# 32x32 turns on VectorE, and the residual added on GpSimd, in the second layer of a two-layer sequence kernel

## The reference, cut to what matters

```python
def _L1_cond_ref(x, c, weight, c_weight, bias):        # x (32,128,2048); 9 taps, 4 groups
    out = lax.conv_general_dilated(x, weight, (1,), [(4, 4)], ..., feature_group_count=4)
    return out + einsum('nd,od->no', c, c_weight)[:, :, None] + bias[None, :, None]
def _L1_ffn_ref(x, up, down, perm):                    # 16 heads of 128 positions, 512 wide inside
    t = x.reshape(b * l, Dm)[:, perm].reshape(b * l, 16, 128)
    t = gelu(einsum('bhd,hdm->bhm', t, up), approximate=False)
    t = einsum('bhm,hmd->bhd', t, down).reshape(b * l, 2048)
    return t[:, unperm]
x = x + _L0_ffn_ref(_L0_cond_ref(x, ...), ...)         # first layer: leaves x1
x = x + _L1_ffn_ref(_L1_cond_ref(x, ...), up, down, perm)
```

## Time and profile before

| | |
|---|---|
| median of 3 runs | 2582.73 us (2581.07 to 2588.96) |
| the profiled execution's own time | 2583.87 us |
| its span, first to last instruction | 2582.0 us |
| TensorE busy | 2528.0 us, 98% of the span |
| VectorE, ScalarE, GpSimd busy | 71%, 39%, 37% |
| second layer, convolution ahead of the heads | about 1470 to 1514 us |
| heads without a last addition | 16 steps, to about 1650 us |
| heads with convolution and last addition | 92 steps, to about 2426 us |
| heads without convolution (`late`) | to about 2548 us |
| last block's sum | to 2582 us |

### The profile page before, as it was taken

The page is one execution under the profiler, slowest core; times in us unless marked ns, Lnnn a source line. Parts: engine busy times, 40 slices in busy tenths (PEclk is TensorE's granted clock), DMA queues, the critical chain, the costliest instruction groups (busy, mean ns, idle before and its releaser), DMA issues.

```text
span 2582.0 us, 39106 instructions
## 1 busy us (share of the span) xinstructions
PE 2528.0 (98%) x12090; PEld 2099.3 (81%) x12090; DVE 1822.8 (71%) x2667; ACT 1001.8 (39%) x1632; POOL 950.8 (37%) x826
## 2 busy tenths in 40 slices
PE   8899999999999999999999999999999999999997
PEld 6788888888888888888888778888888888888775
DVE  6665555965556755576445768888888888888876
ACT  3221212321122322232222555555555555555573
POOL 2366645466654455233223212222222222222231
PEclk9999999999999999999999999999999999999998
DMA  9965644665545777576555754577767676777786
GB/s 318 322 196 199 201 168 155 238 210 197 196 163 185 228 229 228 161 250 210 160 165 186 223 153 131 170 219 219 221 214 226 205 223 205 225 226 223 212 281 240
DMA packets 417281, 541.02 MB, mean 210 GB/s; under 512 B 36248, under 2 KB 270064, under 8 KB 417072
## 3 DMA queue, kind: packets, MB, share of 16 engines
q1 hardware_dynamic: 314816, 307.40, 39.6%
q10 hardware_dynamic: 78144, 154.27, 15.9%
q0 software_dynamic: 24112, 76.80, 9.4%
HBM read 309.72 MB, written 228.61 MB: 208 GB/s over the span
## 4 chain that ended last, share of the span: by engine, by line
PE 91%; DVE 4%; DMA 2%; issue 2%; ACT 1%; ACTq 0%; SPq 0%; POOL 0%; DVEq 0%; POOLq 0%
PE ps_c L461 44%; PE ps_up L1398 13%; PE ps_y L1408 13%; PE ps_c L1423 9%; PE ps_v L439 4%; PE ps_c L427 2%; PE ps_zt L1436 2%; PE ps_f L1444 2%; DVE w_lo L1004 1%; PE ps_up L1423 1%; DVE ring_lo L951 0%; DVE r_early L1000 0%; DMA a_s<-in_lora_a 0%; DMA x_n<-in_up 0%; DMA aggw_d<-agg 0%
## 5 line engine op out<-in xcount | busy, mean ns | idle before, releaser
L461 PE MATMUL ps_c<-w_hi,ring_hi 128*128 128x512 f32 x1792 | 703.8, 393 | 3.8 <-DVE r_early L1000 3.2
L461 PE MATMUL ps_c<-w_hi,ring_lo 128*128 128x512 f32 x1792 | 698.0, 390 | 0.0
L461 PE MATMUL ps_c<-w_lo,ring_hi 128*128 128x512 f32 x1792 | 697.8, 389 | 0.0
L611 ACT ACTIVATE ring_hi<-raw_n 128x512 fp32r<-128x512 f32 x382 | 239.4, 631 | 848.7 <-DVE raw_n L942 235.1
L1380 POOL DMA_INDIRECT y_d<-y_s,idx x128 | 145.7, 1139 | 723.1 <-ACT y_s L1548 689.6
L1505 ACT ACTIVATE kern<-ps_up 128x512 f32<-128x512 f32 x512 | 306.6, 599 | 257.5 <-PE ps_up L1398 245.4
L461 PEld LDWEIGHTS ps_c<-w_hi,ring_hi 128*128 128x128 f32 x1792 | 336.7, 188 | 74.5 <-issue 4.0
L461 PEld LDWEIGHTS ps_c<-w_hi,ring_lo 128*128 128x128 f32 x1792 | 336.4, 188 | 70.2
L461 PEld LDWEIGHTS ps_c<-w_lo,ring_hi 128*128 128x128 f32 x1792 | 336.7, 188 | 67.3
L1622 DVE TENSOR_TENSOR g_lo<-kern,g_hi 128x512 fp32r<-128x512 f32 x512 | 354.5, 692 | 38.2 <-ACT g_hi L1509 21.8
L1000 DVE TENSOR_TENSOR r_early<-ps_c,r_early 128x512 f32<-128x512 f32 x256 | 176.6, 690 | 276.2 <-PE ps_c L461 276.2
(11 more groups left out here) (211 smaller groups left out, 3832.9 us busy)
## 6 DMA issues: line engine op xcount, KB each, us to landing
u_d<-raw_n ACTq DMA_DIRECT2D x64, 512.0 KB, 3.2
x_d<-r_early ACTq DMA_DIRECT2D x128, 256.0 KB, 3.6
raw_n<-u_d SPq DMA_DIRECT2D x64, 512.0 KB, 3.6
x_d<-x_s ACTq DMA_DIRECT2D x126, 256.0 KB, 2.7
u_s<-x_d SPq DMA_DIRECT2D x496, 64.0 KB, 2.2
z_d<-x_s SPq DMA_DIRECT2D x120, 256.0 KB
rear<-y_d SPq DMA_DIRECT2D x112, 256.0 KB
rear<-x_d SPq DMA_DIRECT2D x112, 256.0 KB, 4.0
```

The costliest lines, as they stand in the source:

```text
L461: mm = nc.tensor.matmul(bank, a[:, dc, :], w[k][:, dc, :], start=(first and dc == 0 and n == 0), stop=(dc == 3 and n == 2), skip_group_che ...
L611: nc.scalar.activation(ring_hi[g % RING][:].rearrange("p a n -> p (a n)"), factor(q, k, p), ACT.Copy).then_inc(hi_ready, 1)
```

## The change

TensorE's transposes in the loops of the second layer are taken out. VectorE transposes 32x32 squares in SBUF instead, straight from `z_s` into the tile (`turn_z`) and from the loaded y rows into `results` (`turn_y`). Since such a turn moves nothing between quadrants of partitions, three layouts change with it: the four units of a tile are now the four batches of one group, z and y rows are moved by four transfers of 32 partitions, and the output is written by phase in rows of 512 bytes and brought into order on the host. The addition of x1 becomes a GpSimd instruction, `add_x1`, between the gather and the scatter. For mc = 0 and 2 g_hi is now made by ScalarE in every step, for mc = 1 and 3 by VectorE. ScalarE's write of `z_s` now waits for `zt_ready`, VectorE's turn. VectorE takes `turn_y` before `turn_z`. The last block keeps TensorE's transposes; its 16 results leave in four stores each, two on SyncE and two on ScalarE. Cut to its core:

```diff
-        def by_scalar(k, h, mc):
-            return late(k, h) and mc % 2 == 1
+        def by_scalar(mc):
+            return mc % 2 == 0
@@ conv_unit, final_unit
-            return H * k + h + LEAD, h % 2, SB * k + (h + LEAD) // G, h % G
+            group, batch = divmod((h + LEAD) % H, SB)
+            return H * k + h + LEAD, h % 2, SB * k + SB * ((h + LEAD) // H) + batch, group
-            return H * (k - 1) + h, h % 2, SB * (k - 1) + h // 4, h % 4
+            return H * (k - 1) + h, h % 2, h // 4, h % 4
+        def final_part(dram, k, phase, q):
+            first = SB * (k - 1)
+            return dram[bass.ds(first, SB), :, phase, q * P:(q + 1) * P].rearrange("b c q -> c b q")
+        def z_rows(dram, r, part):
+            return dram.rearrange("(w i r) n -> r i w n", w=WIDE, r=S)[r, :, :, part * C:(part + 1) * C]
@@ load_final (SyncE)
-                sp.dma_start(yt_s[j], y_d[1 - parity][c * 512:(c + 1) * 512, h // 4 * C:(h // 4 + 1) * C]
-                             .rearrange("(l p) r -> p l r", p=P)).then_inc(yt_in[j], 16)
+                rows = y_d[1 - parity].rearrange("(q w i s) n -> q s i w n", q=4, w=4, s=S)[q, phase]
+                for g in range(G):
+                    sp.dma_start(yt_s[j][g * GC:(g + 1) * GC, :].rearrange("p (w n) -> p w n", w=4),
+                                 rows[:, :, g * C:(g + 1) * C]).then_inc(yt_in[j], 16)
                 wait(sp, o_ready, v - 1)
-                sp.dma_start(x1_s[j], x1_d[b, :, :, c * P:(c + 1) * P]).then_inc(x1_in[j], 16)
+                sp.dma_start(x1_s[j].rearrange("p (b q) -> p b q", b=SB),
+                             final_part(x1_d, k, phase, q)).then_inc(x1_in[j], 16)
@@ store_out, store_z (SyncE)
-                sp.dma_start(out[b, :, c * 512:(c + 1) * 512], o_s[j]).then_inc(o_out[j], 16)
+                sp.dma_start(final_part(out, k, phase, q), o_s[j].rearrange("p (b q) -> p b q", b=SB)).then_inc(o_out[j], 16)
-                for w in range(2 if isinstance(u, int) and u == H - 1 else 4):
-                    sp.dma_start(z_d[(parity + ahead) % 2][w * 512:(w + 1) * 512, jb * C:(jb + 1) * C]
-                                 .rearrange("(q r) n -> q r n", r=S), zt_of(*before(k, h, 2))[:, w, :, :]).then_inc(z_out[jb % 2], 16)
+                for r in range(2 if isinstance(u, int) and u == H - 1 else S):
+                    sp.dma_start(z_rows(z_d[(parity + ahead) % 2], r, jb),
+                                 zt_of(*before(k, h, 2))[r * GC:(r + 1) * GC].rearrange("p w b c -> p w (b c)")).then_inc(z_out[jb % 2], 16)
@@ GpSimd, after the gather and ahead of the scatter
+            def add_x1(k, h):
+                v, j, _, _ = final_unit(k, h)
+                n = H // 2 * (k - 1) + h // 2
+                pool.wait_ge(fin_done, v + 1)
+                pool.wait_ge(x1_in[j], 16 * (n + 1))
+                nc.gpsimd.tensor_tensor(o_s[j], o_s[j], x1_s[j], ALU.add).then_inc(o_ready, 1)
@@ TensorE: turn_z and turn_y taken out
-                for w in range(4):
-                    mm = nc.tensor.transpose(ps_zt[:, 0, w * P:(w + 1) * P], z[:, w * P:(w + 1) * P], id_s[:])
-                for l in range(4):
-                    mm = nc.tensor.transpose(ps_f[:, 0, l * P:(l + 1) * P], yt_s[j][:, l, :], id_s[:])
@@ ScalarE
-                    wait(act, zt_done, u - 1 if paired(k, h) else u)
+                    wait(act, zt_ready, u - 1 if paired(k, h) else u)
@@ VectorE
-                nc.vector.tensor_copy(zt_of(k, h)[:, :, :, g * GC:(g + 1) * GC],
-                                      ps_zt[:, 0, :].rearrange("p (w r o) -> p w r o", w=4, r=S)).then_inc(zt_ready, 1)
+                nc.vector.transpose(zt_of(k, h)[:, :, n % SB, :], z_pair[pair_of(k, h)]
+                                    .rearrange("p (w c) -> p w c", w=WIDE)).then_inc(zt_ready, 1)
-                nc.vector.tensor_tensor(o_s[j].rearrange("p (q s) -> p q s", s=S),
-                                        ps_f[:, 0, :].rearrange("p (q s) -> p q s", s=S),
-                                        x1_s[j].rearrange("p s q -> p q s"), ALU.add).then_inc(o_ready, 1)
+                nc.vector.transpose(o_s[j].rearrange("p (b w i) -> p b w i", b=SB, w=4),
+                                    yt_s[j].rearrange("p (w b c) -> p b w c", w=4, b=SB)).then_inc(fin_done, 1)
```

More of the change, by code:

```diff
@@ L1075, in layer1_block @@
         rear = sb("rear", [P, 4, 4 * P])
-        yt_s = [rear[:, j, :].rearrange("p (l r) -> p l r", l=4) for j in range(2)]
-        x1_s = [rear[:, 2 + j, :].rearrange("p (s q) -> p s q", s=S) for j in range(2)]
+        yt_s = [rear[:, j, :] for j in range(2)]
+        x1_s = [rear[:, 2 + j, :] for j in range(2)]
         results = sb("results", [P, 2, 512])
@@ L1254, in load_final @@
             def load_final(k, h, parity):
-                v, j, b, c = final_unit(k, h)
+                v, j, phase, q = final_unit(k, h)
                 if h == 0:
@@ L1327, in _ @@
             finish()
+            for v in range(H):
+                store_last(sp, v, range(2))
             sp.wait_ge(o_out[0], 16 * ((STEPS - H) // 2))
@@ L1372, in step @@
                             gather(k + 1, h + n - H, 1 - parity)
+                if final_exists(k, h, 1):
+                    add_x1(*before(k, h))
                 if exists(k, h, 0):
@@ L1414, in conv @@
                 u, j, b, g = conv_unit(k, h)
-                if isinstance(k, int) and u < G:
+                if isinstance(k, int) and u < H:
                     pe.wait_ge(sh.cwlo_ready, g + 1)
@@ L1449, in step @@
                     conv(k, h)
-                if exists(k, h, LEAD - 1):
-                    turn_z(*before(k, h))
-                if final_exists(k, h, 1):
-                    turn_y(*before(k, h))
                 if isinstance(k, int) and H * k + h == -1:
@@ L1553, in _ @@
             for v in range(H):
-                b, c = last_unit(v)
-                act.wait_ge(last_o, v + 1)
-                act.dma_start(out[b, :, c * 512:(c + 1) * 512], last_sum[v]).then_inc(last_o_out, 16)
-            act.wait_ge(last_o_out, 16 * H)
+                store_last(act, v, range(2, SB))
+            act.wait_ge(last_o_out, 64 * H)
         @block.vector
@@ L1631, in step @@
                         split_weights(n)
+                if final_exists(k, h, 1):
+                    turn_y(*before(k, h))
                 if exists(k, h, LEAD - 1):
-                    take_z(*before(k, h))
-                if final_exists(k, h, 1):
-                    take_final(*before(k, h))
+                    turn_z(*before(k, h))
                 if not lead(k) and exists(k, h, LEAD + 1):
@@ L1727 @@
         args.append(nc.dram_tensor(f"in_{name}", a.shape, mybir.dt.from_np(a.dtype), kind="ExternalInput").ap())
[L1728 removed]
+    out = nc.dram_tensor("out_0_dram", (NB, C, S, Q), F32, kind="ExternalOutput").ap()
     build(nc, *args, out)
     r = run_bass_kernel_spmd(nc, [feed], core_ids=[0])
[L1731 removed]
+    return r.results[0]["out_0_dram"].reshape(NB, C, S, Q).swapaxes(-1, -2).reshape(NB, C, L)
```

112 lines of the change are left out of this document (49 added, 63 removed).

## The result

The changed kernel takes 2621.9 us (median of 4 runs, 2618.9 to 2624.2) against 2582.4 for the kernel before beside it. The ratio of the means is 1.0147, with a 95% interval of 1.0127 to 1.0168. The forecast was faster, 2553; it came out 1.5% slower, just outside the range of 2520 to 2620.

The account below looks back on a forecast made before the run. TensorE was taken as the bound in all three stages, with a VectorE-ScalarE loop taking over mid-stage. From 2583.87 us: -1 -5 -32 +12 +3 -7 +0 = -30, so 2554, 2553 beside the median; own range 2530 to 2575, 8-in-10 range 2520 to 2620.

Parts of the forecast that it names:

- The ring: Middle steps: closed loop through VectorE's turns and ScalarE's z and gelus, 8.08 us a step against 8.43; 92 steps save 32.
- rival 2: Middle steps: dearer turns, 1.08 us each, make the loop 8.82 us and the kernel slower, 2621; chance 0.20.
- d: Length of one 32x32 turn of 128x512 fp32 on VectorE, taken as 0.71 us; it enters the loop's 6.66 + 2d.
- rival 1: All stages: TensorE stays the bound, 88 us less, 2495; needs turns of 0.5 us or less; chance 0.07.
- the second ring: Loop t_lo, up 0 to up 2, gelu 2, rounding, y_s, gelu 3, remainder: 7.7 us, binding in 16 steps without last addition.
- Block starts: Six block starts: z store lands 2.1 us late, now inside the loop; 12 us more in all (5 to 20).
- late landings: Other tiles' z stores, and gathers landing later under output stores of 512 bytes: 3 us more.
- rival 3: Z stores from 32 partitions land in 9.5 us, ordinary tiles 2.2 late, block firsts 3.2 more: +56, 2609; chance 0.13.
- 19 late steps: Last steps, without z or split_x: no ring binds, so TensorE's removed turn saves 0.4 us each, 7 in all.
- 16 steps: Steps without a last addition: from 8.02 to 7.7 us each, 5 us less in all.
- Ahead: While the convolution runs ahead: SyncE's issues take over at 2.49 us a unit; 20 units gain 1 us, not 8.
- Rival 4: GpSimd's addition slows VectorE's remainder by 1.15 us; 2582 if a third of steps meet it, 2640 if all; chance 0.08.

Follow-up runs that it names:

- e2: The changed kernel with each tile's four z stores taken from all 128 partitions, not 32 (rows land in wrong order): 2592.1 us, ratio 1.0029.
- e7: The changed kernel with two tiles for the turned z in place of one: 2601.6 us, ratio 1.0075.
- e14: e12 with y loaded in one transfer of adjacent rows into 128 partitions in place of four (parts in wrong order): 2540.4 us, ratio 0.9838.
- e19: e12 with y loaded in one transfer of rows 8 KB apart into 128 partitions (parts in wrong order): 2539.9 us, ratio 0.9830.
- e4: The changed kernel with turn_z ahead of turn_y on VectorE: 2615.4 us, ratio 1.0124.
- e18: e12 with y in four loads of adjacent rows, each into 128 partitions (parts in wrong order): 2554.1 us, ratio 0.9882.
- e12: e11 with the store of a finished output first in SyncE's step: 2557.1 us, ratio 0.9896.
- e10: e9 with ScalarE rounding the gelus of mc = 1 and 3, not 0 and 2, in all steps: 2565.1 us, ratio 0.9932.
- e11: e9 with ScalarE rounding mc = 1 and 3 in the late steps only: 2559.0 us, ratio 0.9901.
- e8: The changed kernel with two tiles for the turned z and turn_z ahead of turn_y: 2571.1 us, ratio 0.9948.
- e9: e8 with the addition of x1 moved from GpSimd to VectorE, behind turn_y: 2568.4 us, ratio 0.9945.
- e13: e12 with z stored from 128 partitions, y loaded in one and output rows of 2 KB (rows in wrong order): 2530.5 us, ratio 0.9798.
- e5: The changed kernel with GpSimd adding x1 to one column in place of 512: 2618.0 us, ratio 1.0137.
- e1: The changed kernel with ScalarE rounding mc = 1 and 3 in the last 19 steps: 2616.1 us, ratio 1.0125.

## Why the forecast was wrong, point by point

Two steps of the prediction failed: the landing of a z store at a block's start, put at 6.34 us and measured at 9.5, and the late steps, where "no ring binds there" was wrong. The rest came out near.

- **The ring, -32**: right in its mechanism, and 0.09 a step too short. 8.17 for 8.08, turns of 0.70 and 0.67 for 0.71, 0.26 saved in a step for 0.35: 90 steps save 23. The turns weren't dear: rival 2 named 2621, but that its number is the one measured is chance, since it needed d = 1.08. TensorE didn't stay the bound (rival 1; by the second ring's 7.7 it couldn't have, whatever d was). The Trainium skill, page "VectorE: DVE Perf Modes", section "The three transpose paths": an estimate from its figure was 0.71 as well, and this trace agrees (0.67 to 0.71).
- **Block starts, +12, and late landings, +3**: the step that failed. They cost 34 and 10 (the 12 less the 2 of before). The 6.34 to the landing was taken over from the earlier trace rows, from four transfers of 128 partitions, to transfers of 32 with more loads in the queues; it took 9.5 in the mean. 3.1 more in each of six is 19. The store also left later than summed, 5.4 behind t_lo for 5.1, which is 2 more: the row that it was counted from was the latest of the five before. Behind the landing lies more than its length. With z from 128 partitions (e2) the block starts still cost 24, with no wait for z at all (e7) 27, since turn_y then waited for the output store. Only one load of y in place of four (e14, e19) brought them to nothing, on top of the second tile, the two changes of order and the addition on VectorE. So it is rival 3 in the landing time (9.5, as it said), but the 32 partitions are only about 10 of the 34, and the last 12 to 16 went only with fewer transfers behind the store. The other 17 tiles were milder than rival 3 had them: nine waited, 0.2 to 1.3 each for 2.2, until e4 made nearly all wait. By the Trainium skill, page "SBUF — State Buffer", section "Door 1: The DMA port swizzle", 32 partitions reach half of the ports: for z stores e2 agrees (issues 3.6 against 2.6, the time 30 less); for loads of y e18 against e12 doesn't show it (3 us).
- **19 late steps, -7**: failed, +11. Two mistakes. The earlier trace rows was read as "TensorE is the bound", but its turn lay in the wait for y_s; taking it away gains nothing (e10, e11: 6.19), which is the 7. And "no ring binds there" left out that the moved rounding stands ahead of y_s; the chain gelu 2, rounding, y_s was in the prediction as the second ring, yet was applied only where 16 steps were counted. It made the step 6.80, 0.6 longer, which is the 11; e11 shows it, and that GpSimd's addition would have done the same.
- **16 steps, -5**: -3 (7.82 for 7.7). The mechanism was right: in the step below gelu 2 waits for TensorE and starts 3.73 after up 0, where 3.6 had been put, and the other terms are as added up. e8 and e9 show the same 7.83 once the first ring is opened.

```profile
1613.36 0.50 PE L1431 MATMUL ps_up<-t_hi,w_hi 128*128 128x512 f32 x1
...
1617.09 0.60 ACT L1514 ACTIVATE kern<-ps_up 128x512 f32<-128x512 f32 x1 [0.22 <-PE ps_up L1431]
```

- **Ahead, -1**: +5. The 0.65 per issue of a z store from the earlier trace rows became 0.9, a microsecond more for each of five tiles. With z from 128 partitions the stage took 60.0 (e2) and 57.4 (e13), for 62.9.
- **Rival 4**: an addition stops VectorE 1.1 to 1.7 us in each late step, but its price hangs on what else is late: nothing in the changed kernel (e5), and 0.6 a step once the rounding is out of the way (6.77 in e1, 6.19 in e11). In the middle steps it lies beside turn_z, which it didn't lengthen (0.71 at most).
- **Rest**: the forecast's 30 less and the result's 40 more differ by 70: 37 in the middle, 18 late, 6 ahead, 2 in the 16 steps, 1 in the end, and 6 that lie ahead of the first z.

With the turns e11 and e12, which leave nothing out, take 1.0% less than the kernel before. What the other edits would have given without the turns was not run. The turns needed a second z tile, another order on VectorE, the addition on VectorE and ScalarE's rounding chosen by stage.

## What to carry to other kernels

Taking work from the busiest engine gains nothing where that engine would have waited just then: look for what follows the removed instruction, and whether its input was there. When a wait moves from an engine with slack into a closed ring, the landing time of its transfer has to be priced anew with its new shape and its new neighbours in the queue, not read off the old one. A second buffer takes that wait away, and the next one behind the same queue may take its place (27 of 34 us stayed); fewer transfers took them all away. And two limits of nearly the same length must be lifted together: alone they gave 6 and 20 us, together 51.
